# A Flamingo-style decoder step on one core: group weights by one matmul per batch, column maxima without GpSimd, context sums between the projections

## What is computed

```python
x = x + tanh(g_xattn[0]) * linear_attention(layernorm(x), ctx)      # 16 heads, 64 context rows, gated
x = x + tanh(g_ffn[0])   * (gelu(layernorm(x) @ W1.T + b1) @ W2.T + b2)
x = x + tanh(g_xattn[1]) * softmax_readout(layernorm(x), ctx)
x = x + tanh(g_ffn[1])   * expert_ffn(layernorm(x))

# expert_ffn: 32 experts' probabilities give each token a weight for each of 8 groups
w_tg = einsum('tk,tkg->tg', top_val, onehot)
act = silu(gate) * up                                   # of each group's dominant expert
out = einsum('tg,tgh->th', w_tg, einsum('tgi,ghi->tgh', act, dn))
```

## Time and profile before

| | us |
|---|---|
| median of 3 runs | 1888.39 (1887.68 to 1888.73) |
| profiled execution | 1887.19 |
| its span | 1885.4 |
| TensorE busy | 1846.4 |
| VectorE busy | 995.9 |
| ScalarE busy | 538.6 |
| GpSimd busy | 323.5 |
| mean granted clock of TensorE | 0.993 of full |

### The profile page before, as it was taken

How to read it: one execution, slowest core, us unless ns; L and a number is a source line. 1 busy time by engine, 2 the same in 40 slices (tenths; PEclk the granted TensorE clock), 3 DMA queues, 4 the chain that set the end, 5 groups by cost and what they waited for, 6 DMA issues and landing times.

```text
span 1885.4 us, 24612 instructions
## 1 busy us (share of the span) xinstructions
PE 1846.4 (98%) x9552; PEld 905.6 (48%) x9552; DVE 995.9 (53%) x2036; ACT 538.6 (29%) x801; POOL 323.5 (17%) x299
## 2 busy tenths in 40 slices
PE   8799999999999999999999999999999999999999
PEld 3445554644444444444444444444444444444444
DVE  5676776754554455454436554545445455554422
ACT  3224433312221122122112233233333223333321
POOL 1123322222021120202010011111111111111111
PEclk9899999999999999999999999999999999999999
DMA  5124433333414223340310200101010101000000
GB/s 159 55 62 129 140 118 95 96 129 65 104 42 127 90 68 104 70 125 27 90 54 9 76 1 23 32 1 54 1 54 1 54 1 54 1 23 1 1 23 23
DMA packets 135830, 112.10 MB, mean 59 GB/s; under 512 B 75554, under 2 KB 92066, under 8 KB 135714
## 3 DMA queue, kind: packets, MB, share of 16 engines
q1 hardware_dynamic: 135714, 110.53, 19.7%
HBM read 78.00 MB, written 32.51 MB: 59 GB/s over the span
## 4 chain that ended last, share of the span: by engine, by line
PE 83%; issue 9%; DVE 3%; POOL 2%; DMA 2%; ACT 1%; POOLq 0%; SPq 0%; DVEq 0%; ACTq 0%
PE bank L923 44%; PE bank L1012 17%; PE bank L1092 10%; PE bank L992 4%; PE bank L932 3%; PE bank L977 1%; POOL arena L897 1%; PE bank L958 1%; PE bank L1079 1%; PE bank L1027 1%; POOL arena L871 0%; PE bank L1054 0%; DVE arena L1278 0%; DMA arena<-in_L_xattn_Wkv 0%; DMA arena<-x_after_ffn 0%
## 5 line engine op out<-in xcount | busy, mean ns | idle before, releaser
L923 PE MATMUL bank<-arena 128*128 128x512 f16 x4608 | 1042.2, 380 | 8.4 <-DVE arena L1299 7.3
L923 PEld LDWEIGHTS bank<-arena 128*128 128x128 f16 x4608 | 451.1, 98 | 538.9 <-DVE arena L1299 7.8
L1012 PE MATMUL bank<-arena 128*128 128x512 f16 x1536 | 352.1, 379 | 1.2 <-DVE arena L1506 1.2
L1092 PE MATMUL bank<-arena 128*128 128x512 f16 x1152 | 264.3, 379 | 0.9 <-POOL arena L897 0.9
L1648 DVE SCALAR_TENSOR_TENSOR arena<-bank,arena 128x512 f32<-128x512 f32 x96 | 72.0, 750 | 329.0 <-PE bank L923 329.0
L1191 ACT ACTIVATE arena<-bank,arena 128x512 f32<-128x512 f32 x128 | 99.5, 778 | 493.5 <-PE bank L923 490.5
L1012 PEld LDWEIGHTS bank<-arena 128*128 128x128 f16 x1536 | 150.1, 98 | 181.1 <-DVE arena L1506 1.7
L897 POOL TENSOR_TENSOR arena<-arena 128x512 f16<-128x512 f32 x96 | 111.0, 1157 | 626.0 <-ACT arena L1228 626.0
L1504 DVE TENSOR_SCALAR arena<-arena 128x512 f16<-128x512 f32 x128 | 65.8, 514 | 281.6 <-ACT arena L1191 281.3
L1092 PEld LDWEIGHTS bank<-arena 128*128 128x128 f16 x1152 | 112.0, 98 | 128.4 <-POOL arena L897 1.4
L1506 DVE SCALAR_TENSOR_TENSOR arena<-arena 128x512 f16<-128x512 f32 x128 | 118.0, 922 | 4.6
(11 more groups left out here) (159 smaller groups left out, 1215.8 us busy)
## 6 DMA issues: line engine op xcount, KB each, us to landing
arena<-in_L_ffn_proj SPq DMA_DIRECT2D x64, 256.0 KB, 2.9
arena<-in_L_ffn_gate_up_proj SPq DMA_DIRECT2D x96, 96.0 KB, 2.0
x_after_attention<-arena SPq DMA_DIRECT2D x8, 1024.0 KB, 5.2
arena<-x_after_attention SPq DMA_DIRECT2D x8, 1024.0 KB, 5.6
x_after_ffn<-arena SPq DMA_DIRECT2D x8, 1024.0 KB, 4.3
arena<-x_after_ffn SPq DMA_DIRECT2D x8, 1024.0 KB, 6.2
arena<-in_x SPq DMA_DIRECT2D x7, 1024.0 KB, 5.5
normalised_blocks<-arena SPq DMA_DIRECT2D x28, 256.0 KB, 2.0
```

Source lines behind the costliest of these rows:

```text
L923: m = e.matmul(bank[b][:, :], wT[l][:, c, tile * P:(tile + 1) * P], y[h][:, c, :], start=n == 0, stop=n == NPASS - 1)
L1012: m = e.matmul(bank[t][:, :], hv[h][:, 0, t * P:(t + 1) * P], w2T[l][:, j, :], start=j == 0 and i == 0, stop=j == NH - 1 and i == 2)
L1092: m = e.matmul(bank[t][:, :], hv[h][:, 0, t * P:(t + 1) * P], dnT[l][:, j, :], start=j == 0 and i == 0, stop=j == NR - 1 and i == 2)
```

## The change

**Group weights.** One matmul per batch (`gsum`) with a stationary operand of 64 x 128, of which the first 8 columns say which expert belongs to which group, gives the 8 groups' weights of all 512 tokens in 8 rows. ScalarE scales the 8 rows into gsum_s, SP stores them in DRAM (`group_weights`), and SP loads each group's row back as a broadcast to 128 partitions into gw_s (`gload`). The loads of a batch's first two groups stand at the end of the batch before, ahead of the store of that batch's x; those of the very first batch stand in its first steps. The load of a later x moves from behind the store to step 3. `attention_tasks` is taken three times in a step, with pauses between its parts.

**Maxima over partitions.** GpSimd's `partition_all_reduce` is gone. TensorE turns the column of 128 maxima into a row (`allt`, one transposition), VectorE takes the row's maximum, TensorE spreads it over 128 partitions by a matmul with a column of ones (`allb`), and VectorE copies it out.

**Order in stage A.** The four `kvsum` steps stand between q and gate tiles of batch 0 and not behind all of them, `numden` of batch 0 between gate tiles. The tables, b1's maximum and the context's stand between batch 0's output tiles. **In stage F** the layer norm's block tasks are cut in pairs, with fewer empty slots between.

```diff
+    def over(kind, name):
+        add(kind, name, banks=1)
+
+    def over_partitions(name):
+        over("allt", name)
+        late.append(lambda: (over("allb", name), late.append(lambda: after_max(name))))
...
     add("kvv", 3, banks=1)
+    over("allt", "g")
     add("keysv", 2)
...
     for j in range(NC):
         add("q", 0, j, banks=1)
         if j == 0:
             add("keysv", 3)
+            over("allb", "g")
             add("pow", "g")
             split("g")
+            add("vmax")
+            add("all", "v")
+        else:
+            add("kvsum", j - 1, banks=4)
+        if j == 1:
+            over("allt", "v")
+        if j == 2:
+            over("allb", "v")
...
             norms.pop(0)()
             add("out", b - 1, t, banks=1)
+            if b == 1 and t == 0:
+                add("tables")
+                add("all", "b1")
+                add("ctxmax")
+                add("all", "c")
...
             for gg in range(j * P // INTER, ((j + 1) * P - 1) // INTER + 1):
-                if gg * INTER >= j * P:
-                    add("bw", b, gg, banks=1)
+                if gg * INTER >= j * P and (b == 0 or gg > 1):
+                    add("gload", b, gg)
             add("mix", b, j)
...
-                if bd + 3 < NB:
-                    add("xload", "E", bd + 3)
+        if J < total and j == NR - 1 and b + 1 < NB:
+            add("gload", b + 1, 0)
+            add("gload", b + 1, 1)
+        if J < total and j == 3 and 0 < b < NB - 2:
+            add("xload", "E", b + 2)
...
+            elif kind == "gsum":
+                b = step[1]
+                w.wait_ge(gs_ok, nth[step])
+                e.dma_start(gscr[b], gsum_s[0:NG, :]).then_inc(gs_out, 16)
+            elif kind == "gload":
+                _, b, gg = step
+                m = nth[step]
+                w.wait_ge(gs_out, 16 * (b + 1))
+                if m <= 3:
+                    w.wait_ge(down_mm, DN2 * NB)
+                else:
+                    w.wait_ge(mixed, mix_last(m - 3))
+                e.dma_start(gw_s[(m - 1) % 3], gscr[b, gg].partition_broadcast(P)).then_inc(gw_in[(m - 1) % 3], 16)
...
-            elif kind == "all":
-                ap = sc["m" + step[1]]
-                w.wait_ge(all_in, n)
-                e.partition_all_reduce(ap, ap, P, bass.bass_isa.ReduceOp.max).then_inc(all_out)
...
+                e.transpose(bank[k][0:1, 0:P], sc["m" + step[1]], ident).then_inc(all_turned)
...
+                e.matmul(bank[k][:, 0:1], onesP[0:1, :], row[step[1]][0:1, :], start=True, stop=True).then_inc(all_spread)
```

More of the change, by code:

```diff
@@ L156, in weights_until, with block_tasks, stats, tile @@
             flush()
+    def block_tasks(i):
+        def stats(ts):
+            for t in ts:
+                add("stat", i, t)
+            if NT - 1 in ts:
+                add("rs", i)
+        def tile(t):
+            add("norm", i, t)
+            add("block", i, t)
+            add("bstore", i, t)
+            if t == NT - 1:
+                add("bload", i)
+        def whole(cs):
+            for c in cs:
+                add("whole", i, c)
+        return ([lambda: stats((0, 1)), lambda: stats((2, 3))] + [lambda t=t: tile(t) for t in range(NT)]
+                + [None] * 3 + [lambda: whole((0, 1)), lambda: whole((2, 3)), None])
     def ln_tasks(i, apart=False):
@@ L242, in make_plan @@
             add("keysv", 3)
+            over("allb", "g")
             add("pow", "g")
             split("g")
-        flush()
+            add("vmax")
[6 more added lines that the diff above has]
+            over("allb", "v")
+        flush()
+        if j == 2:
+            add("consts")
+            add("pow", "v")
+        if j > 1:
+            norm(2)
     scaled.update("qg")
-    add("consts")
     add("xload", "A", 2)
-    norms = ln_tasks(("A", 1), apart=True)
     for j in range(NC):
         add("gate", 0, j, banks=1)
-        norm()
         if j == 0:
[L254 to L257, removed]
-        weights(N_O)
[L259 to L271, removed]
+            add("kvsum", 3, banks=4)
+        else:
+            add("numden", 0, j - 1, banks=2)
+        if j < 2:
+            norm()
+        weights(N_O)
+    norm()
+    add("numden", 0, NT - 1, banks=2)
+    norm(3)
+    weights(N_O)
+    weights(N_O)
     owed = [0.0]
@@ L306, in make_plan @@
             add("out", b - 1, t, banks=1)
+            if b == 1 and t == 0:
[3 more added lines that the diff above has]
+                add("all", "c")
+            if b == 1 and t in (1, 2):
+                over("allt" if t == 1 else "allb", "b1")
+                over("allt" if t == 1 else "allb", "c")
+            if b == 1 and t == 3:
+                add("pow", "c")
             if b < NB - 1:
@@ L327, in make_plan @@
     weights_until(N_B)
[L329 to L346, removed]
     P_.ring, P_.turn = [4, 5, 6, 7], 0
@@ L408, in make_plan, with apart @@
     while side:
-        side.pop(0)()
+        f = side.pop(0)
+        if f:
+            f()
     add("xload", "E", 1)
     add("xload", "E", 2)
+    def apart():
+        f = side.pop(0) if side else None
+        if f:
+            f()
     total = NB * NR
@@ L517, in build @@
     wmax = small(64)
+    row = {n: small(1) for n in ("c", "v", "b1", *SIZE)}
     gains, tanhg = small(4), small(4)
@@ L1073, in tensor_program @@
                 project(step, upT, j, yT[b % 2], ue_mm)
[L1074 to L1075 removed]
+            elif kind == "gsum":
+                b = step[1]
                 k = bank_free(step)
[L1077 removed]
+                w.wait_ge(r_copied, n)
                 w.wait_ge(dconst, 13)
[L1079 removed]
+                e.matmul(bank[k][:, :], of_group, wTs[b % 2], start=True, stop=True).then_inc(gs_mm)
             elif kind == "dn":
```

93 lines of the change are left out of this document (57 added, 36 removed).

## The result

The changed kernel takes 1912.00 us (median of 4 runs, 1908.80 to 1914.06) against 1888.25 us (4 runs, 1887.68 to 1888.73) for the kernel before: ratio 1.0124, 95% interval 1.0111 to 1.0136. It is slower by 23.8 us, outside the range of 1873 to 1892, and on the other side of the forecast of 1883.6. The profiled execution took 1911.25 us with a span of 1909.5, 24.1 above the 1885.4 of before.

What follows compares the result with a forecast made beforehand. TensorE, busy 1846.4 of 1885.4 us, was taken as the bound. Terms -12.1 + 7.7 - 7.0 + 2.1 - 5.0 + 9.5 = -4.8 us gave span 1880.6, stated as 1883.6 us for the runs' median; range 1873 to 1892.

Steps and rivals of the forecast that it cites:

- VectorE bounds the opening: Rival: every further opening step hangs on VectorE's order; batch 2 later than 137.5 us means slower or the same; chance 0.2.
- Part 1: Expert batches: 64 group-weight matmuls become 8, each dropped one saving a wide matmul's pitch; -12.1 us.
- Part 2: Expert stage's start: first broadcast lands late behind 3 MB of transfers; 5.1 us stop plus 2.6 for the clock, +7.7.
- The rival of transfers that interleave: Small transfers pass large ones, so the first broadcasts cost 0 and the time is 1875.9 us; chance 0.08.
- Part 3: Opening, first q projection to batch 2: the new order moves the losses; -7 us (-12 to +2), batch 2 at 132.5.
- the stop at g's maximum: Ahead of the first q projection: TensorE waits for g's maximum, 5 us and 2.6 for the clock.
- Part 4: Maxima of the remaining weights: matrix 1 +2.1, matrix 2 -5.0, gate, up, d and router together +9.5 us.
- Matrix 1: Its turning and spreading pair stands behind the numerators, where VectorE ends later than TensorE; +2.1 us.
- Gate and up: Feed-forward: pair behind an up projection, 2.3 us stop and 0.3 work each, 5.2 together, plus 1 each for the clock.
- d: Feed-forward: its maximum uncovers only part of VectorE's delay, down steps cover the rest; 0.9 us.
- Matrix 2: Its pair costs 2.1 us, but the 4.30 us stop at 297.45 and its clock give back 7.1; net -5.0.
- The rival that they belong to the powers: GpSimd's 7 us stops belong to its one-lane powers, so the stop at 297.45 stays: +7.1, 1890.8 us; chance 0.05.

Runs made afterwards that it cites:

- lead: Changed kernel with tile maxima held at o's last tile until all of o is split, so loads stand tiles ahead again; 1889.09 us, ratio 1.0009.
- bgone: Kernel before, with tile maxima running on while o is not yet split, so each load stands directly ahead of its maximum; 1925.50 us, ratio 1.0192.
- nolead: Changed kernel with turning and spreading apart, first group weights before x's store, g's turning after the first q projection, maxima still running ahead; 1886.81 us.
- gfirst: Changed kernel with the first three group-weight broadcasts, then x's load for expert batch 1, issued ahead of the store of x; 1912.07 us.
- lead_gfirst: Kernel of lead with SP's order first broadcast, x's load for expert batch 1, two more broadcasts, then the store of x; 1882.41 us.
- poolmax: Kernel of lead with first group weights before x's store, but partition maxima back on GpSimd and TensorE's turnings and one-column matmuls gone; 1892.60 us.
- apart: Changed kernel with the spreading matmul three weights' steps behind the turning instead of one, from matrix 1 to the router; 1904.38 us.

## Why the prediction was wrong

**The step that failed** is in parts 3 and 4: they price the maxima of q and g and those of matrix 1 onwards, and have no term for o's, neither for its pair (a stop of 1.47 us ahead of batch 1) nor, above all, for what stands behind it in the order of the weights. Of a moved step every queue that it is moved past counts. o's splits were moved past the point at which maxima of matrix 1 may begin, and these then ran ahead of the loads. The prediction has no term for VectorE waiting on `in_L_ffn_proj`; there was no such wait in the trace of before, and the sentence on DMA queues spoke only of the expert stage. It was to be read from the order alone: a load three tiles ahead of its maximum on the one side, directly ahead on the other. The price was in the trace too, with 2.9 us for a 256 KB load against a VectorE that is busy 30.71 of 47 us in the opening. Runs lead, bgone and nolead give it as 22.9, 37 and 23.1 us. One of the prediction's signs of being wrong stood there too: batch 2 was to start between 127 and 140, and started at 146.97.

**The rival came out on the right side with the wrong mechanism.** "VectorE bounds the opening" said that batch 2 later than 137.5 means slower. It was 146.97, and it was slower. But with the lead put back VectorE has the same work, and batch 2 starts at 132.22. That the time came out on this side is luck. A busy share is no reason for a bound; the row to look at is what the engine waits for.

**Part 1, group weights, -12.1:** right. The expert stage takes 822.4 us before and 810.2 in nolead, in which its start is mended: 12.2.

**Part 2, the first broadcasts, +7.7:** right in place and mechanism, near in size. The product is at 1104.62, 11.2 us behind the first load of x of 1093.40, where 1076.2 - 1064.46 = 11.7 were expected; the stop 4.79 us for 5.1 predicted, with the slow clock behind it (4.33 us for twelve, 1.6 lost instead of 2.6). The expert stage as a whole: -4.8, predicted -4.4. The Trainium skill ("DMA: Bandwidth & Descriptors", queues, rings and completion order) has descriptors taken in ring order on each DMA engine; gfirst agrees in both directions, since the broadcast ahead of x came without a wait and x behind it 2.81 us late. The rival of transfers that interleave fell: the broadcast behind 3 MB did not come early. In lead_gfirst the other order won back 7.9 us of the stage.

**Part 3, the opening, -7.0:** its sum was right to 0.3 us once the cause above is taken out (132.22 against 132.5); in the changed kernel it was hidden behind +7.5. That closeness is partly luck, as two errors cancel: in run lead batch 1 starts at 89.82 and not at 88, with o's pair and its stop of 1.48 us ahead of it, and is then 2.1 us shorter than predicted (42.4 us against 44.5), since the tables and the context's maximum stop TensorE for 0.88 us and not for 3. Of its pieces the stop at g's maximum was foreseen and is there, 3.86 us:

```profile
45.94 0.37 PE L1010 MATMUL bank<-arena 128*1 128x128 f32 x1 [3.86 <-DVE arena L1383]
```

The first q projection starts at 46.11 (45.4 predicted), batch 1 at 90.35 (88).

**Part 4.** Matrix 1: a stop of 1.69 us for 2.1 in sum; in run lead another 1.7 for the clock. Gate and up: 2.35 us each for 2.3. d: 2.68 for 0.9, the term that was mis-sized most, because the turning itself waits for VectorE, not only the spreading. Router: 0.73 and 0.46 for 1.4. The feed-forward part together +11.3 for +9.5. Matrix 2: in run lead the 4.30 us stop is gone, as predicted, but 1.11 and 2.64 us of new ones stand in its place; all of the first stage is 5.2 us shorter there and not 9.9.

**What the sum would have been:** run lead is the change with that one cause taken out, and it measures 1889.1, 5.5 above the forecast and inside the range. It is no faster than the kernel before (ratio 1.0009), so the gain that was forecast didn't come there either. 22.9 of the 28.4 us by which the forecast missed are the one overlooked step; the rest is matrix 2, d and the clock.

**The removal:** GpSimd's stops by "issue" ahead of and behind its maxima are gone, as predicted. The 13 us for each of the 12 were too wide a reading, though: in the trace of before the 5.8 to 6.4 us ahead stand by themselves at three maxima, at the others GpSimd waited for something else meanwhile, and of two maxima in a row (97.42 and 99.61) the second starts 1.83 us after the first. The rival that they belong to the powers falls: the powers are still there, and poolmax has the stops back, 7.93 us ahead of a maximum and 7.52 behind it. The Trainium skill ("GPSIMD Engine Reference", wrapper-ucode dispatch) gives some 6 us for the first call after code is freshly loaded. The stops of 5.8 to 7.9 us ahead of the maxima agree or lie above it, late in the kernel too; those of 6.9 us and more on the way back to ordinary operations it doesn't speak of. The trace of before has a row for it that the prediction passed over, instructions on the maxima's line that change GpSimd's configuration, 18 for the 12 maxima (count, ns min/median/max, first and last start):

```profile
L856 POOLq MODIFY_POOL_CONFIG  x18: 1/8/20, 22.4 to 868.9; - x18
```

The changed kernel has none. That the stops are code being loaded is not shown; the rows show only that these instructions and the stops come and go together.

## What to carry to other kernels

When an edit delays one step, follow what it releases: here a chain of splits, the buffers that they free, and the loads that fill them. Count, for each load, how many uses stand between it and its own use before and after the edit; if the number goes to zero, up to the full latency of the load (3 us here, at ten of 32 tiles) enters the order of the engine that uses it, however idle the DMA engines are. And put a pair of small dependent matmuls as far apart as the work between them lets you: moving the second one by two steps took stops of 2.35 us out, and the kernel was 7.6 us faster (run apart).

## What was not expected of the hardware

- The same stop, 2.35 us on TensorE at the same instruction, lowered the clock in one kernel (twelve matmuls in 4.38 us) and not in another (2.76 us). At matrix 1 it is 1.69 us in the changed kernel with the clock left up, and 1.70 us in lead with twelve matmuls in 4.45 us behind it. The prediction took 1 us for each such stop, between 0 and 2.6. It can't be had more closely from one trace: the feed-forward part of lead and of lead_gfirst, with the same steps, lasts 685.1 and 690.4 us, and in lead_gfirst twelve matmuls take 4.45, 4.17 and 4.38 us behind the stops at gate, up and d. It need not be the same in each execution of one kernel: that profiled execution took 1886.55 us at a mean granted clock of 0.992, the other five of lead_gfirst 1880.53 to 1883.50 us at 0.995. In the changed kernel the stops of 3.86, 4.79, 10.15 and 13.19 us all lowered it.
- Where GpSimd waits for nothing else, it stops 5.8 to 7.9 us between other work and a partition maximum, and 6.9 to 8.3 us between the maximum and its next ordinary operation (before and poolmax), late in the kernel as at its start.
